# Sub-expert down products in blocks of six tiles, a later load order for their weights, and the linear products of fusion and gates issued before the third step

## The reference

```python
lin_out = jnp.einsum('bsd,bde->bse', qf, kv) / (normalizer[..., None] + 1e-06)
gate = jax.nn.sigmoid(jax.nn.relu(gate_in @ W_g1 + b_g1) @ W_g2 + b_g2)
fused = gate * lin_out + (1.0 - gate) * win_out
return fused @ W_out + b_out + residual
```

```python
z = jnp.einsum('nd,sdr->nsr', xf, P)
scores = jnp.einsum('nsr,smr->nsm', z, C)
topv, topi = jax.lax.top_k(scores, K)
w = jax.nn.softmax(topv, axis=-1)
h = jax.nn.gelu(jnp.einsum('nsr,nskrh->nskh', z, W1g) + b1g)
yl = jnp.einsum('nskh,nskhr->nskr', h, W2g) + b2g
comb = jnp.einsum('nskr,nsk->nsr', yl, w)
out = jax.nn.gelu(comb.reshape(xf.shape[0], S * R) @ G1 + g1b) @ G2 + g2b
```

## Time and profile before

| | us |
|---|---|
| median of 3 runs | 2113.61 |
| lowest, highest | 2112.82, 2124.57 |
| profiled execution, in all | 2136.09 |
| its span, first to last instruction | 2134.4 |

### The profile page before, as it was taken

One profiled execution on the slowest core, in us unless ns is written; L12 is line 12 of the kernel. 1 busy time (PEld: TensorE's weight loads), 2 busy tenths in 40 slices (PEclk: granted clock), 3 DMA queues, 4 the chain that ended last, 5 costly groups with the idle time before them and its releaser, 6 DMA issues. The chain is left out here.

```text
span 2134.4 us, 38683 instructions
## 1 busy us (share of the span) xinstructions
PE 1827.5 (86%) x13920; PEld 1324.6 (62%) x13920; DVE 1221.3 (57%) x3653; ACT 836.5 (39%) x1667; POOL 378.5 (18%) x377
## 2 busy tenths in 40 slices
PE   5999969977775999788898775999999899768997
PEld 3688759956664898577655542333333688546886
DVE  1468842238998222567635454788888576792221
ACT  1245413314541111245435545677667355311111
POOL 1100112243212331421001011000000000123443
PEclk8989979998995999789998787999999999888999
DMA  5000345510004554102000114900000000304662
GB/s 198 1 1 0 119 136 186 181 49 14 12 4 149 184 186 129 28 15 85 0 1 17 36 40 138 299 2 1 1 1 1 24 1 0 131 22 119 181 184 64
DMA packets 83838, 156.75 MB, mean 73 GB/s; under 512 B 22389, under 2 KB 57941, under 8 KB 82805
## 3 DMA queue, kind: packets, MB, share of 16 engines
q1 hardware_dynamic: 63669, 134.71, 19.4%
q0 software_dynamic: 19552, 19.63, 3.8%
q10 hardware_dynamic: 480, 0.63, 0.1%
HBM read 125.04 MB, written 29.48 MB: 72 GB/s over the span
## 5 line engine op out<-in xcount | busy, mean ns | idle before, releaser
L2375 DVE TENSOR_TENSOR l2s_gated<-l2s_hidden,ps 128x408 f32<-128x408 f32 x512 | 262.6, 574 | 59.3 <-PE ps L2280 59.0
L2345 ACT ACTIVATE l2s_hidden<-ps,pack_l2f 128x816 f32<-128x816 f32 x256 | 226.9, 937 | 99.2 <-PE ps L2272 98.5
L129 PE MATMUL ps<-pack_const 128*128 128x512 bf16 x508 | 147.1, 429 | 28.7 <-PEq L163 15.0
L2280 PE MATMUL ps<-l2s_gs,l2s_spread 96*128 96x408 bf16 x512 | 150.8, 340 | 0.3 <-DVE l2s_gated L2375 0.3
L2272 PE MATMUL ps<-l2s_zs,l2s_up 128*128 128x408 bf16 x512 | 132.7, 341 | 15.3 <-DMA l2s_down<-in_sub_down 15.3
L1895 PE MATMUL ps<-l_down,l_hidden 128*128 x792 | 139.8, 326 | 0.0
L1895 PEld LDWEIGHTS ps<-l_down,l_hidden 128*128 128x128 f32 x792 | 127.3, 190 | 0.4
L2290 PE MATMUL ps<-l2s_gated,l2s_down 128*32 128x408 f32 x1024 | 114.3, 518 | 4.0 <-DVE l2s_comb L2362 3.7
L2272 PEld LDWEIGHTS ps<-l2s_zs,l2s_up 128*128 128x128 bf16 x512 | 39.6, 97 | 120.2 <-ACT l2s_hidden L2345 82.2
L1854 POOL DMA_INDIRECT l_xt<-rows_in,l_tokens x66 | 63.1, 956 | 255.7 <-PE ps L1867 197.0
L129 PEld LDWEIGHTS ps<-pack_const 128*128 128x128 bf16 x508 | 50.5, 108 | 90.1 <-issue 59.1
(11 more groups left out here) (470 smaller groups left out, 3950.9 us busy)
## 6 DMA issues: line engine op xcount, KB each, us to landing
l_up<-in_l_up SPq DMA_DIRECT2D x66, 576.0 KB, 3.9
l3c_wg<-in_l_gate SPq DMA_DIRECT2D x16, 576.0 KB
l3c_wu<-in_l_up SPq DMA_DIRECT2D x16, 576.0 KB
l3c_wd<-in_l_down SPq DMA_DIRECT2D x16, 576.0 KB
slots_out<-l_y SPq DMA_DIRECT2D x66, 96.0 KB
l_down<-in_l_down SPq DMA_DIRECT2D x8, 675.0 KB, 9.5
g_parts<-l2b_g_parts SPq DMA_DIRECT2D x12, 408.0 KB, 4.3
l_down<-in_l_down SPq DMA_DIRECT2D x8, 576.0 KB, 7.3
```

What stands on the lines that cost most here:

```text
L129: pe.matmul(bank, halves[:, 0:128], halves[:, :], start=True, stop=True)
L2280: pe.matmul(gate_bank(n), spread[:, t % 8, :], gs[half][2 * r + odd][:, t // 8, pair, chunk(n % 2), :], start=True, stop=True).then_inc(ga ...
L2345: act.activation(hidden[:, p % kept, :, :], ps[:, 0, 2 * (p % 2):2 * (p % 2) + 2, 0:NG], ACT.Gelu_apprx_tanh, bias=w.at("b1")[:, s * MT + ...
L2375: dve.tensor_tensor(gated[:, n % ring, :], hidden[:, n // 2 % kept, n % 2, :], gate_bank(n), ALU.mult)\
```

## The change

In fusion and gates TensorE issues `lin_outputs`, and VectorE `lin_results` and `fuse`, before `step(at[2])` and no longer after it. ScalarE's order stays.

In the sub-experts the down products are issued in blocks of three pairs (six tiles); the last two blocks of each 64 pairs have two pairs (four tiles). `cuts` holds the first pair of each block and `blocks` maps the last pair of a block to its first; a block is issued, as before, after the gate spreads of the pair two behind its last one. Up and down weights have semaphores of their own: the up products wait for the up weights, and the first down product of a k for the down weights. SP's order becomes, for each k of the first half: z, up weights, (for k = 0) the spread matrix, the gate parts, down weights.

```diff
--- before.py
+++ after.py
@@ -1340,9 +1340,9 @@
                     lin_scores(q)
                 if 1 <= q <= G:
                     gate_products(q - 1)
-                step(at[2])
                 if q < G:
                     lin_outputs(q)
+                step(at[2])
                 if 1 <= q <= G:
                     fused_transposes(q - 1)
                 step(at[3])
@@ -2177,10 +2177,13 @@
 
     w = g["l2f"]
     ps, h = g["ps"], g["h"]
-    gates, kept, group, ring = 3, 3, 4, 10
+    gates, kept, ring = 3, 3, 10
     order = [(half, r, odd, t, pair) for half in range(2) for r in range(2) for odd in range(2)
              for t in range(MT) for pair in range(2)]
     pairs, per_sum_bank = len(order), len(order) // 2
+    cuts = [bank * per_sum_bank // 2 + at for bank in range(4) for at in (*range(0, per_sum_bank // 2 - 4, 3),
+                                                                        per_sum_bank // 2 - 4, per_sum_bank // 2 - 2)]
+    blocks = {last - 1: first for first, last in zip(cuts, cuts[1:] + [pairs])}
     with ExitStack() as stack:
         m = Memory(nc, g, stack, "l2s")
         up_parts = [m.sb(f"up{k}", [128, 2, NM * 32], BF16) for k in range(4)]
@@ -2196,7 +2199,7 @@
         up_ps, gate_ps = m.sem("up_ps"), m.sem("gate_ps")
         hid_ready, gated_ready = m.sem("hid_ready"), m.sem("gated_ready")
         comb_ps, comb_ready, comb_added = m.sem("comb_ps"), m.sem("comb_ready"), m.sem("comb_added")
-        weights_loaded = [m.sem(f"weights_loaded{k}") for k in range(4)]
+        up_loaded, down_loaded = ([m.sem(f"{name}_loaded{k}") for k in range(4)] for name in ("up", "down"))
         parts_loaded = [[m.sem(f"parts_loaded{half}{k}") for k in range(4)] for half in range(2)]
         spread_loaded, spread_ready, sums_loaded = m.sem("spread_loaded"), m.sem("spread_ready"), m.sem("sums_loaded")
         pack_loaded = m.sem("pack_loaded")
@@ -2228,13 +2231,16 @@
 
         @block.sync
         def _(sp):
-            def weights(k):
+            def up_weights(k):
                 first = 4 * (k // 2) + k % 2
                 sp.dma_start(up_parts[k][:, :, :], g["up_pairs"][first:first + 3:2, :, :].rearrange("s k n -> k s n"))\
-                  .then_inc(weights_loaded[k], 16)
+                  .then_inc(up_loaded[k], 16)
+
+            def down_weights(k):
+                first = 4 * (k // 2) + k % 2
                 sp.dma_start(down[k][:, :, :, :].rearrange("p s t r -> p s (t r)"),
                              dram["sub_down"].rearrange("p (s n) -> p s n", s=NS)[:, first:first + 3:2, :])\
-                  .then_inc(weights_loaded[k], 16)
+                  .then_inc(down_loaded[k], 16)
 
             def parts(half, k):
                 first = 4 * (k // 2) + k % 2
@@ -2242,15 +2248,18 @@
                 sp.dma_start(zs[half][k][:, :, :, :],
                              g["z_pairs"][first:first + 3:2, :, there, :].rearrange("s k b l -> k s b l"))\
                   .then_inc(parts_loaded[half][k], 16)
-                if half or k:
-                    gate_parts(sp, half, k)
-
-            sp.dma_start(spread_raw, dram["sub_spread"]).then_inc(spread_loaded, 16)
+
             for half in range(2):
                 for k in range(4):
                     parts(half, k)
                     if not half:
-                        weights(k)
+                        up_weights(k)
+                    if not half and not k:
+                        sp.dma_start(spread_raw, dram["sub_spread"]).then_inc(spread_loaded, 16)
+                    if half or k:
+                        gate_parts(sp, half, k)
+                    if not half:
+                        down_weights(k)
                     if not half and k == 2:
                         sp.dma_start(comb[:, :, :, :, :], g["sub_bias"]).then_inc(sums_loaded, 16)
                         sp.dma_start(per_sum[:, :, :, :, :], g["sub_per_sum"]).then_inc(sums_loaded, 16)
@@ -2264,7 +2273,7 @@
                 k = 2 * r + odd
                 if t == 0 and pair == 0:
                     if not half:
-                        pe.wait_ge(weights_loaded[k], 32)
+                        pe.wait_ge(up_loaded[k], 16)
                     pe.wait_ge(parts_loaded[half][k], 16 * 7)
                 if p >= 2:
                     pe.wait_ge(hid_ready, p - 1)
@@ -2280,16 +2289,20 @@
                 pe.matmul(gate_bank(n), spread[:, t % 8, :], gs[half][2 * r + odd][:, t // 8, pair, chunk(n % 2), :],
                           start=True, stop=True).then_inc(gate_ps, 1)
 
-            def second(n):
-                if n % per_sum_bank == 0 and n:
-                    pe.wait_ge(comb_ready, n // per_sum_bank)
-                pe.wait_ge(gated_ready, n + group)
-                for at in range(n, n + group):
+            def second(p):
+
+                first, n = 2 * blocks[p], 2 * p + 2
+                if first % per_sum_bank == 0 and first:
+                    pe.wait_ge(comb_ready, first // per_sum_bank)
+                pe.wait_ge(gated_ready, n)
+                for at in range(first, n):
                     half, r, odd, t, pair = order[at // 2]
+                    if not half and t == 0 and pair == 0 and at % 2 == 0:
+                        pe.wait_ge(down_loaded[2 * r + odd], 16)
                     row = HP * (2 * (at % 2) + pair)
                     last = pe.matmul(sums[row:row + HP, :], down[2 * r + odd][:, pair, t, :], gated[:, at % ring, :],
                                      start=(odd == 0 and t == 0), stop=(odd == 1 and t == MT - 1))
-                if (n + group) % per_sum_bank == 0:
+                if n % per_sum_bank == 0:
                     last.then_inc(comb_ps, 1)
 
             def hidden_products(q):
@@ -2320,9 +2333,9 @@
                     up_products(p + 1)
                 for n in (2 * p, 2 * p + 1):
                     gates_spread(n)
-                if p >= 3 and p % 2 == 1:
-                    second(2 * p - 6)
-            second(2 * pairs - group)
+                if p - 2 in blocks:
+                    second(p - 2)
+            second(pairs - 1)
             fill(pe, g, ps[:, 0, 2, :], 8)
             pe.wait_ge(comb_ready, 4)
             hidden_products(0)
@@ -2367,7 +2380,7 @@
                 dve.tensor_tensor(h[:, four, :], h[:, four, :], w.at("g2b").unsqueeze(1).broadcast_to([L, GB, D]), ALU.add)\
                    .then_inc(based, 1)
             for n in range(2 * pairs):
-                if n > per_sum_bank and n % per_sum_bank == group + 2:
+                if n > per_sum_bank and n % per_sum_bank == 6:
                     dve.wait_ge(sums_loaded, 32)
                     add_sums(n // per_sum_bank - 1)
                 dve.wait_ge(gate_ps, n + 1)
```

## The result

The changed kernel takes 2145.95 us (median; 2140.55 to 2148.74), beside 2115.56 us for the kernel before on the same chip. The ratio is 1.0117, 95% interval 1.0090 to 1.0143: slower by 25 us, 19 to 30. The plain medians of the four runs each lie 30 us apart, at the upper end of this. The forecast was +27 us.

What follows compares the result with a forecast made beforehand. TensorE's order, in series with VectorE's first multiply, was taken to bound the sub-experts, and a chain of waits between engines fusion and gates. +37 + 0 - 10 = +27 us on 2113.6 gave 2141 us, range 2110 to 2156.

Steps and rivals of the forecast that it cites:

- Rounds and block: Sub-experts' down products: six tiles on four places take four rounds, so a block costs 1.51 us instead of 0.83.
- Rivals B: Sub-experts: doubled places cost in proportion, block 1.17 us, stage +10, fusion -10, total 2114 us; chance 0.13.
- D: Sub-experts: tiles five and six do not overlap each other, two more rounds, block 2.19 us, total 2195; chance 0.06.
- The period: Sub-experts: VectorE's wait stays in series with the block; 4.17 us per six tiles against 3.71 before, +37 us in all.
- Rival C: Sub-experts: saved block switches reach the end, 10 us, VectorE's wait absorbed, with fusion -10: 2094 us; chance 0.05.
- Bank changes: Sub-experts' three sum-bank changes: the block loses its 1.25 us wait, the sixth spread still waits; 0 us (bounds -4 and 0).
- The loads: Sub-experts' entry: first up product moves 0 to -2 us, VectorE's start 0 to +1.5; taken as 0 (bounds -2, +1.5).
- Fusion: Fusion and gates: VectorE's step 3 starts earlier at q = 2, 3, 4; -10 us (bounds -12.5 and -4).
- three leads: Fusion and gates: VectorE's step 3 starts 3.4, 3.3 and 3.1 us earlier at q = 2, 3 and 4.
- Rival E: Fusion and gates: the reorder gives nothing or loses, leaving +37 alone, 2151 us; chance 0.04.
- The sum: Whole kernel: +37 (blocks) + 0 (loads) - 10 (fusion) = +27 us on median 2113.6, giving 2141 us.

Runs made afterwards that it cites:

- kernel with two places: Kernel before, blocks of four, with each block's four tiles all sent to two places, so its output differs: 2220.86 us in one run, +85 us.
- second profile of the changed kernel: The changed kernel unaltered, run again beside its two parts on one chip, against the kernel before: ratio 1.0098 (1.0067 to 1.0129), +21 us.

## Why the prediction was right, point by point

**Rounds and block: right.** 4, 4, 2, 2 records, 1.50 us against 1.51. The kernel with two places and the one with blocks of eight show the cause: a place takes its products one after the other, a round costs 0.34 us full or half full. Rivals B (1.17) and D (2.19) fall with it. The Trainium skill (TensorEngine Tiling (Array Packing), Key Properties) says that different tiles run in parallel. The traces agree for different places, where four records start within 0.02 us, and show the limit: two products for one tile don't.

**The period: mechanism right, size 0.05 too long.** VectorE's wait stays on the path with 1.09 us of idle time (forecast about 1.0), but the period is 4.12, not 4.17. The term that was mis-sized is the two more multiplies at 0.51 each; in a row they follow each other at 0.49, and only the last one shows its full length. Over 80 blocks that is 4 us, and nearly all of the difference between the forecast +37 and the measured +32.2 from first to last block. Rival C, the 10 us of switches reaching the end, didn't come: VectorE's wait and the rounds outweigh them, and the blocks of eight, with full rounds and 60 blocks fewer, are no gain either. (By the rows 0.10 and 0.12 a block's two ends cost 0.22, not the 0.25 used, so the 10 were 9.)

**Bank changes: right.** TensorE at the second bank:

```profile
1402.91 0.52 PE L2281 MATMUL ps<-l2s_zs,l2s_up 128*128 128x408 bf16 x2
...
1404.82 0.35 PE L2289 MATMUL ps<-l2s_gs,l2s_spread 96*128 96x408 bf16 x1 [1.21 <-DVE l2s_gated L2388]
1405.09 1.56 PE L2303 MATMUL ps<-l2s_gated,l2s_down 128*32 128x408 f32 x12
```

The block no longer waits; the sixth spread does, 1.21 us where the block waited 1.25. Each change costs about 1.1 us instead of 1.3: -0.7 in all, inside the bounds -4 and 0.

**The loads: right in sum, with more inside.** The entry, as in the earlier trace rows:

```profile
1296.52 2.97 ACTq L2228 DMA_DIRECT2D l2s_gs<-g_parts  x6
...
1306.46 1.06 ACT L2352 ACTIVATE l2s_spread<-l2s_gated 96x1024 bf16<-96x1024 f32 x1 [13.09 <-DMA l2s_gated<-in_sub_spread]
...
1306.97 1.52 PE L2281 MATMUL ps<-l2s_zs,l2s_up 128*128 128x408 bf16 x4 [13.17 <-DMA l2s_gs<-g_parts]
...
1307.55 3.57 DVE L2380 TENSOR_TENSOR h<-h,pack_l2f 102x768 f32<-102x768 f32 x4 [22.13 <-ACT l2s_spread L2352]
...
1311.03 2.04 DVE L2388 TENSOR_TENSOR l2s_gated<-l2s_hidden,ps 128x408 f32<-128x408 f32 x4
```

From ScalarE's first gate-part issue to the first up product it is 10.45 us; before it was 12.55, so -2.1, just beyond my 0 to -2. ScalarE can convert the spread matrix only at 1306.46, and VectorE gains nothing: its first multiply comes 14.51 us after that issue, 14.49 before. This varies between profiles of the same code; in the second profile of the changed kernel it is 15.54, within my +1.5. The first block stands 19.67 after the issue, 18.06 before. I had not put this +1.6 into the sum: the first block is due a pair later. With the blocks alone it is 19.19, so that about 1.1 of the 1.6 is the later block.

**Fusion: mechanism right, gain larger than forecast.** The timeline at q = 2, beside the earlier trace rows:

```profile
1112.41 1.56 PE L1198 MATMUL ps<-rows_z 102*102 102x193 f32 x8
...
1116.41 0.96 DVE L1544 TENSOR_TENSOR rows_z<-rows_z,o_all 102x768 f32<-102x768 f32 x1
...
1117.83 0.86 PE L1243 MATMUL ps<-pack_const,rows_z 102*96 102x102 f32 x8
...
1122.38 0.54 ACT L1456 ACTIVATE l2b_g_parts<-pack_l0a 128x408 bf16<-128x408 f32 x1 [0.47 <-DVE pack_l0a L1606]
1122.83 0.89 ACT L1392 ACTIVATE pack_l0f<-ps 96x408 f32<-96x408 f32 x2
...
1124.46 1.11 DVE L1579 MAX8 l2b_best<-x 102x8 f32<-102x64 f32 x8 [1.51 <-ACT x L1414]
```

Laid on the times of before (add 17.89, so that the bias product sums L1535 coincide), TensorE issues the linear outputs at 1130.30 (forecast 1130.3), the fusion ends at 1135.26 (1135.3). Two links of the chain then go faster than I put them. ScalarE ends step 2, the one at `at[2]`, at 1140.81, 1.7 us late and not 2.1. The first scores of step 3, at `at[3]`, come 1.6 us after the start of ScalarE's copies (1122.83 to 1124.46), where I had 2.1. VectorE gets to step 3 4.4 us earlier than before, not 3.4, with 1.51 us idle instead of 4.37. At q = 3 and 4 it is 4.9 and 4.6 (each laid on L1535 of its own q), which is more than the idle time there (4.22 and 3.94) that I had taken as the upper bound. VectorE's timeline at q = 3 says why. Before, the first scores of step 2 had a wait too:

```profile
1190.76 1.11 DVE L1579 MAX8 l2b_best<-x 102x8 f32<-102x64 f32 x8 [2.05 <-ACT x L1414]
```

In the changed kernel, the linear results, the same point, and the first scores of step 3:

```profile
1171.17 0.23 DVE L1507 TENSOR_SCALAR rows_z<-ps 102x2 f32<-102x2 f32 x2 [1.37 <-PE ps L1198]
...
1174.73 1.10 DVE L1579 MAX8 l2b_best<-x 102x8 f32<-102x64 f32 x8
...
1183.23 1.11 DVE L1579 MAX8 l2b_best<-x 102x8 f32<-102x64 f32 x8 [0.18 <-ACT x L1414]
```

Results and fusion now fill the 2.05 us ahead of step 2, at a new wait of 1.37 us for TensorE's linear outputs, and the wait of step 3 shrinks from 4.22 to 0.18. My bound counted one idle time where the edit reaches two. L1243's waits of 5.26, 2.77 and 3.42 us are gone; the one left, 1.28, was there before. The stage gains 12.7 us in this profile, 10.7 to 14.0 over the profiles with this edit, against -10 forecast.

But the three leads don't add up to that gain, as the forecast had it. From L1535 of q = 2 to that of q = 3 the changed kernel takes 56.3 us instead of 57.0, from there to q = 4 52.4 instead of 58.7, and from there to the end of the stage 72.2 instead of 76.2: 0.7, 6.3 and 3.9, together 11.0, where I had 3.4, 3.3 and 3.1. Most of the first lead of 4.4 is gone a round later; why, no run shows. The other 1.7 us of the 12.7 lie at the start of the stage, up to L1535 of q = 1 (41.9 us instead of 43.6, at a granted clock of 0.92 instead of 0.88), where the edit moves no work of a step. In both profiles of the fusion edit alone that start is 43.6 as before, and the gain is 10.7. So the mechanism and the sum of -10 held, but not the division among the three rounds; that the three errors nearly cancel is luck. Rival E, no gain from this edit, falls with its two measurements (-15 and -14).

**The sum.** +32.2 (loop) + 1.6 (first block) - 12.7 = +21, against +27 forecast; on the median 2113.61 that would be about 2135. The misses in the period (-4) and in fusion (-3, with the 1.7 at the stage's start) have one sign, that of the first block (+1.6) the other. Both +21 and +27 lie in the intervals of the two timed comparisons (19 to 30 and 14 to 28). In this profile another 5.5 us at the end of the sub-experts come on top; they are the subject of the last section. So that the forecast +27 lies so near the +25 of the first comparison is in part luck: what the traces tie to the edits is +21.

## What to carry to other kernels

Count a batch of column-tiled products by the longest queue on one place, not by the number of tiles: six tiles on four places cost as much as eight. Where such a block stands in an in-order stream that feeds another engine, put it between two products for which that engine already holds its other input, so that it works on the first during the block and gets the second right behind it; that gave 18 us here, while making the block larger gave none. Before merging blocks to save switches, write out the chain of one period and see whether a wait is there to take the saving.

## What the runs showed of the hardware

In the changed kernel's profile the sub-experts' end took 19.9 us instead of 14.3 after the last block. The row 1670 to 1686 of the stretches above has a granted clock of 0.57, near the 1.2 GHz level, with TensorE busy 14.71 of 16 us. The profile with the fusion edit alone shows the same:

```profile
1652.00:1668.00 16.00, 14.71 (x40) 8.84 (x40) 5.89 (x13) 1.19 (x2) 1.50 (x4) 0.56 0.04 6
```

In the kernel before, 1665 to 1675 stood at 1.00. The clock of this tail fell in three profiles (changed kernel, fusion edit twice) and not in the second profile of the changed kernel, nor in the other kernels' (14.3 us in nine of these ten, the kernel before among them; 16.4 with the doubled places, whose blocks are longer). So the same kernel has it or not. All three are profiles with the fusion edit, of which there are seven; of the six without it none has it. That may be chance, and the runs don't exclude that the edit makes it likelier. What ahead of it makes the clock fall I can't say. The same holds for the stretch before fusion and gates, 1028 to 1050 us long over these profiles with the same code in it, and for fusion and gates itself, 273.9 to 279.2 us in the six profiles without the edit. Single profiles of this kernel therefore differ by 5 to 22 us in places that the edit doesn't touch, as much as the effect looked for.
